# Image 1's returned rows on two DMA queues, and two of its six sums on POOL

## The reference, cut to what matters

```
t = _to_tokens(x)                     # x: (2, 128, 48, 48) -> (2, 2304, 128)
t = t + _L1_ffn_ref(_ln_t(t), gate_w, gate_b, w1, w2, w3)
x = _from_tokens(t, x)
return x
```

## Time and profile before

| what | before |
|---|---|
| runs | 684.36, 678.06 and 683.85 us, median 683.85 us |
| profiled execution | 683.36 us, of which the span from the first to the last instruction is 681.3 us |
| mean granted TensorE clock | 0.905 |
| busy time: PE, POOL, DVE, ACT | 554.9, 408.2, 348.6, 342.1 us |
| chain that ended last, by engine | PE 56%, DVE 14%, POOL 9%, ACT 7%, DMA 3% |
| DMA moved | 72.15 MB |

### The profile page before, as it was taken

One profiled execution on the slowest core, in us unless ns is written; L12 is line 12 of the kernel. 1 busy time (PEld: TensorE's weight loads), 2 busy tenths in 40 slices (PEclk: granted clock), 3 DMA queues, 4 the chain that ended last, 5 costly groups with the idle time before them and its releaser, 6 DMA issues.

```text
span 681.3 us, 15719 instructions
## 1 busy us (share of the span) xinstructions
PE 554.9 (81%) x5422; PEld 468.6 (69%) x5423; DVE 348.6 (51%) x1021; ACT 342.1 (50%) x801; POOL 408.2 (60%) x468
## 2 busy tenths in 40 slices
PE   2477788778779999999999999959649729999960
PEld 2466667657547777677777678748639729999960
DVE  6977787846620171212001274784875405555563
ACT  4467668886547243674122552522515406666640
POOL 1568789767567388675333330037747777777771
PEclk9689999979869699999999988978978959999995
DMA  8452322212055455322219200001123123333457
GB/s 296 161 140 82 85 73 81 67 47 70 13 180 201 154 174 171 128 94 99 88 47 331 61 1 1 0 23 52 52 61 98 52 85 99 98 97 98 128 204 242
DMA packets 56288, 72.15 MB, mean 106 GB/s; under 512 B 9086, under 2 KB 46934, under 8 KB 55614
## 3 DMA queue, kind: packets, MB, share of 16 engines
q1 hardware_dynamic: 49374, 58.36, 27.5%
q0 software_dynamic: 5120, 10.57, 4.7%
q10 hardware_dynamic: 1728, 2.36, 0.9%
HBM read 55.83 MB, written 21.69 MB: 114 GB/s over the span
## 4 chain that ended last, share of the span: by engine, by line
PE 56%; DVE 14%; POOL 9%; issue 9%; ACT 7%; DMA 3%; SPq 1%; POOLq 0%; DVEq 0%; ACTq 0%
PE bank L836 12%; PE bank L798 9%; PE bank L781 8%; PE bank L902 7%; PE bank L847 6%; POOL gathered_or_att L580 3%; POOL padded_or_w L571 3%; ACT normed L947 2%; POOL gathered_or_att L589 2%; PE bank L325 2%; DVE ln_stats L1133 2%; PE bank L796 2%; PE bank L827 2%; PE bank L733 2%; PE bank L867 1%
## 5 line engine op out<-in xcount | busy, mean ns | idle before, releaser
L615 POOL TENSOR_TENSOR padded_or_w<-padded_or_w,gathered_or_att 128x384 f32<-128x384 f32 x96 | 95.4, 1000 | 80.7 <-ACT padded_or_w L1021 77.0
L632 POOL DMA_INDIRECT sorted_x<-normed,slot x72 | 71.2, 989 | 80.0 <-DVE slot L1395 51.4
L1021 ACT ACTIVATE padded_or_w<-bank,moe_b 128x384 f32<-128x384 f32 x96 | 55.3, 579 | 107.2 <-PE bank L781 107.1
L651 POOL DMA_INDIRECT returned<-gathered_or_att,home_of_slot x88 | 87.2, 991 | 26.8 <-issue 19.8
L798 PEld LDWEIGHTS bank<-moe_or_conv,padded_or_w 128*128 128x128 f32 x576 | 80.6, 197 | 30.9 <-issue 9.8
L798 PE MATMUL bank<-moe_or_conv,padded_or_w 128*128 128x128 f32 x576 | 83.9, 284 | 0.0
L781 PE MATMUL bank<-chan_major,moe_or_conv 128*128 128x384 f32 x192 | 82.7, 517 | 0.1
L671 PE MATMUL bank<-padded_or_w 64*64 64x64 f32 x1152 | 47.5, 233 | 27.3 <-issue 15.9
L1459 DVE TENSOR_TENSOR att_or_moe<-att_or_moe,bank 128x256 f32<-128x256 f32 x88 | 37.0, 420 | 61.2 <-ACT att_or_moe L1035 39.9
L671 PEld LDWEIGHTS bank<-padded_or_w 64*64 64x64 f32 x1152 | 41.5, 145 | 36.6 <-issue 32.8
L580 POOL TENSOR_TENSOR gathered_or_att<-gathered_or_att,score_max 128x384 f32<-128x384 f32 x48 | 39.9, 830 | 34.5 <-DVE score_max L1217 33.7
(11 more groups left out here) (214 smaller groups left out, 1122.8 us busy)
## 6 DMA issues: line engine op xcount, KB each, us to landing
gathered_or_att<-combine SPq DMA_DIRECT2D x24, 768.0 KB, 4.2
padded_or_w<-windows SPq DMA_DIRECT2D x192, 48.0 KB, 2.0
sorted_x<-in_pad_rows SPq DMA_DIRECT2D x22, 260.0 KB, 7.1
padded_or_w<-sorted_x SPq DMA_DIRECT2D x22, 260.0 KB
padded_or_w<-in_moe_w SPq DMA_DIRECT2D x8, 512.0 KB, 5.4
qy<-returned SPq DMA_DIRECT2D x6, 384.0 KB, 5.8
out<-residual ACTq DMA_DIRECT2D x12, 192.0 KB, 2.1
normed<-returned SPq DMA_DIRECT2D x6, 384.0 KB, 5.4
```

What stands on the lines that cost most here:

```text
L615: nc.gpsimd.tensor_tensor(HB[n % DRING], HB[n % DRING], GB_[k % 3][:, n % 4, :], ALU.mult).then_inc(S("gated"), 1)
L632: nc.gpsimd.indirect_dma_start(xs_dram, bass.IndirectOffsetOnAxis(ap=POS[b][:, k, t:t + 1], axis=0), TNR[b][:, t, :], None).then_inc(S(don ...
L651: nc.gpsimd.indirect_dma_start(yt_dram, bass.IndirectOffsetOnAxis(ap=HOMES[b][:, j:j + 1], axis=0), YR[k * RING + j % RING], None).then_in ...
L1021: nc.scalar.activation(HB[n % DRING], banks[HBANK[n % 2]][:, 0:DG], ACT.Gelu, bias=B1C[:, e:e + 1]).then_inc(S("gelu"), 1)
```

## The change: what it does

Only image 1's end is changed; image 0's loads, sums and stores are issued as before.

- SP issues the loads of groups 0, 2 and 4 alone. The loads of groups 1, 3 and 5 are issued by ACT, at the beginning of `store(1)`, so behind image 0's stores and ahead of image 1's. For that ACT now has the nine waits of `y_rows_out` too, and one for the scatter of image 1, since the loads go into the tile that this scatter reads.
- Groups 2 and 5 are summed by POOL in place of DVE, in a new phase behind POOL's last indirect DMA: the same two additions, with a wait for itself between them.
- DVE leaves these two groups out, and ACT waits for a second semaphore, `out_ready_pool`, ahead of their stores. The stores are issued in the order of the groups, as before.

```diff
+        BY_POOL = (2, 5)
+        def returned_group(b, g):
+            return yt_dram[2 * NT * b:2 * NT * (b + 1), :].rearrange("(p g n) c -> g p (n c)", g=NG, n=2 * TG)[g]
...
-                rows = yt_dram[2 * NT * b:2 * NT * (b + 1), :].rearrange("(p g n) c -> g p (n c)", g=NG, n=2 * TG)
-                for g in range(NG):
-                    sp.dma_start(YL[b][g], rows[g]).then_inc(S(f"y_back{b}{g}"), 16)
+                for g in range(0, NG, 1 + b):
+                    sp.dma_start(YL[b][g], returned_group(b, g)).then_inc(S(f"y_back{b}{g}"), 16)
...
+            def combine(b):
+                for g in BY_POOL if b else ():
+                    xt = XT[b][:, g * TG:(g + 1) * TG, :].rearrange("p t c -> p (t c)")
+                    pool.wait_ge(S(f"y_back{b}{g}"), 16)
+                    nc.gpsimd.tensor_tensor(xt, xt, YL[b][g][:, 0:DG], ALU.add).then_inc(S("half_sum"), 1)
+                    pool.wait_ge(S("half_sum"), BY_POOL.index(g) + 1)
+                    nc.gpsimd.tensor_tensor(xt, xt, YL[b][g][:, DG:2 * DG], ALU.add).then_inc(S("out_ready_pool"), 1)
...
             def store(b):
+                if b:
+                    act.wait_ge(S("scattered1"), 16 * TT)
+                    y_rows_out(act, b)
+                    for g in range(1, NG, 2):
+                        nc.scalar.dma_start(YL[b][g], returned_group(b, g)).then_inc(S(f"y_back{b}{g}"), 16)
                 for g in range(NG):
-                    act.wait_ge(S("out_ready"), b * NG + g + 1)
+                    by_pool = [h for h in BY_POOL if b and h <= g]
+                    if g in by_pool:
+                        act.wait_ge(S("out_ready_pool"), len(by_pool))
+                    else:
+                        act.wait_ge(S("out_ready"), b * NG + g + 1 - len(by_pool))
                     nc.scalar.dma_start(out[b, :, g * TG:(g + 1) * TG, :], XT[b][:, g * TG:(g + 1) * TG, :]).then_inc(S("out_stored"), 16)
...
             def combine(b):
                 for g in range(NG):
+                    if b and g in BY_POOL:
+                        continue
```

More of the change, by code:

```diff
@@ L652, in send_back @@
                                                  YR[k * RING + j % RING], None).then_inc(S(f"y_sent{k}"), 16)
-            run(A=lambda n: attend(att, n), TO=toeplitz, AN=add_normed, D=dense, XC=pad, RS=scatter, M=send_back)
+            def combine(b):
[5 more added lines that the diff above has]
+                    nc.gpsimd.tensor_tensor(xt, xt, YL[b][g][:, DG:2 * DG], ALU.add).then_inc(S("out_ready_pool"), 1)
+            run(A=lambda n: attend(att, n), TO=toeplitz, AN=add_normed, D=dense, XC=pad, RS=scatter, M=send_back, F=combine)
         @block.tensor
```

## The result

The changed kernel took 696.25 us (median of 4 runs, 689.02 to 699.11) against 682.88 us for the kernel before (4 runs): a ratio of 1.0184, 95% interval 1.0138 to 1.0231. Forecast were 683.6 us and 677.8 to 685.8. Measured once more, with 11 runs against 28, it was 1.0077 (1.0039 to 1.0115), +5.3 us. So the change costs time, and the two measurements differ in how much. Executions over 1.5% above the fastest of their kernel are left out of the ratios and kept in the medians.

What follows compares the result with a forecast made beforehand. Bound by image 1's loads until group 3, three groups on DVE and one store; last store issued at 678.8 in place of 679.0 us, then 2.3 us unchanged: -0.2 us, 683.6 us against the median, range 677.8 to 685.8.

Steps and rivals of the forecast that it cites:

- What bounds the kernel, and the 13.3 us that can be touched: From SP's first load of image 1 (668.0 us) to the span's end (681.3): loads, DVE's sums, one store; 2% of span.
- Loads issued by two engines: Image 1's loads: SP's last issue comes 1.4 us earlier, worth nothing by itself; ACT's three issues cost 3 x 0.34 us.
- Stores behind loads: Image 1's stores queue behind ACT's loads: loads keep about 415 GB/s, groups land in pairs, the last 1.6 us earlier.
- The two engines beside each other: POOL's sums beside DVE's: each POOL addition takes 0.17 us more, 1.11 us, and the chain ends at 678.8 us.
- the first rival: POOL's and DVE's sums of image 1 exclude one another: +1.4 us, 685.2 us; chance 0.20.
- POOL's last indirect DMA ends ahead of all this, and nothing is queued behind the sums: POOL's sums of groups 2 and 5: POOL is free before them and has no work after; group 5 would end at 678.2.
- from there to the end stay 2.3 us: From the last store's issue (678.8 in place of 679.0 us) to the kernel's end: unchanged at 2.3 us.
- The chance of 0.92 for a change within 1%: Whole kernel: chance 0.92 that the time stays within 1% (6.8 us), with 0.04 each for faster and slower.

Runs made afterwards that it cites:

- loads alone: Changed kernel with all sums on DVE, image 1's loads still issued by SP and ACT; 680.73 us against 682.64 for the kernel before, ratio 0.9973.
- the changed kernel with the added DRAIN: Changed kernel plus one DRAIN on POOL directly behind its last indirect DMA, ahead of its sums; 24.1 us from PE's last DRAIN to the end.
- an early DRAIN: Changed kernel plus one DRAIN on POOL ahead of image 1's scatter; 29.7 us from PE's last DRAIN to the end.

## Why the prediction was wrong, point by point

- *What bounds the kernel, and the 13.3 us that can be touched:* right up to the last store, wrong behind it. I read the end off the chain of waits. The chain of the kernel before did name POOL's DRAIN, in one line among POOL's last operations, and I passed over it:

```profile
659.61 1.36 POOLq L60
```

  The line gives the 1.36 us that lie on the chain and not the 15.68 that the DRAIN lasts; only the operations of line 60 show its end.
- *Loads issued by two engines:* right. SP and ACT issue together (671.2 and 671.3 us), at no cost that shows.
- *Stores behind loads:* right in the rate, wrong in the order, and worth less than I took it for. The rate holds. But the groups do not come in pairs: in the changed kernel SP's three loads land ahead of ACT's (us from issue to landing; first line SP's, second ACT's):

```profile
DMA to landing us min/median/max: 4.2/5.7/7.2
```
```profile
DMA to landing us min/median/max: 4.9/7.3/8.0
```

  Group 2 starts on POOL 677.4 - 671.2 = 6.2 us after the first load, as forecast (674.2 - 668.0), but group 3 starts on DVE 7.8 us after it, where I had it land together with group 2 and start at 6.5. Group 5 was in 680.2 - 671.2 = 9.0 us after the first load, where I had 8.1 and before it was 9.7. What the loads alone are worth hardly shows: from the first load to the end of DVE's last sum it is 10.4 us in both profiles of loads alone, and 10.5 to 11.0 in the five with all loads on SP and all sums on DVE. The Trainium skill, in "DMA: Bandwidth & Descriptors" (section "Issuing engines are not separate DMA queues"), lets a second issuer save only the issuing time. The times agree with that within their scatter (ratio 0.9973, with 1 in its interval). Whether the steadier rate comes from the order on ACT's queue or from the second issuer, no run tells.
- *The two engines beside each other:* mis-sized. I took 0.17 us more for each of POOL's additions and none that matters for DVE's. POOL's mean is 1.13 us against the 1.11 forecast, which is luck, since that price came from indirect DMAs. DVE's four additions take nearly twice as long, DVE ends last, and the last store comes 0.9 to 1.3 us later in place of 0.2 earlier. That is close to the first rival's +1.4 us, but part of it is group 3, which that rival has on time. From 679.05 to 683.10 us four additions of DVE and two of POOL begin, and 0.5 us are left of an earlier one of POOL: one after another they would take 4 x 0.545 + 2 x 0.94 + 0.5 = 4.6 us, side by side 2.2, and 4.05 passed. When POOL's four stood beside DVE's four, in the changed kernel with the added DRAIN, they took 5.2 us (683.24 to 688.45) against 5.9 in turns. So the engines mostly take turns here, as the Trainium skill says in "SBUF — State Buffer" (section "Who interferes with whom"), but by these times the exclusion is not quite whole.
- *"POOL's last indirect DMA ends ahead of all this, and nothing is queued behind the sums":* this step failed, and with it *"from there to the end stay 2.3 us"*. POOL's DRAIN was queued behind, 8.7 us long; before, it had ended 5.8 us ahead of SP's, and now it ends 5.8 us behind. It costs 5.9 us of the 7.9. That POOL "has nothing behind its last indirect DMA", as the description of the kernel has it, is true of the operations that the kernel writes and not of the end of its program.
- *The chance of 0.92 for a change within 1%:* it rested on the claim that a loss of 1% would need sums of twice their length. Every part that I named was bounded; the part that decided was not among them. By the tails (+6.8 to +7.9 us) the loss is about 1%, most of it not from the sums, and by the second measurement (0.77%) it would still count as within 1%: the change lies near the edge of that band, and the first measurement beyond it.

Open are two things. What a DRAIN works off, and why 8.7 us: it is long only behind indirect DMAs, is paid once, and neither their number nor an early DRAIN gives its length. And the first measurement's 12.6 us: the tail explains 6.8 to 7.9 of it. In the one of these four runs that has a profile, the work ahead of PE's DRAIN took 2.5 us more than in the profile before (661.1 against 658.6 us), though the change doesn't touch it. The two longest runs, of 698.8 and 699.1 us, have granted clocks of 0.892 and 0.878 and no profile, so that where their time went is not shown. In the second measurement, of 5.3 us, there is no such rest.

## What to carry to other kernels

Before work is moved to an engine that finishes early, look at what that engine still has to do after its last operation, and whether the time is covered: here an idle engine had 5.8 us to spare and not the 14.5 us that its last operation suggested (666.6 to 681.1 us). Ask for the lines on which the program's end is booked, and compare the end of the chain with the end of the span; when they part by more than the last store takes (2.3 us before, 8.6 after), look behind the last operation. And take additions of DVE and POOL that both read two operands from SBUF as work mostly in turns, not side by side.

## What the hardware did that I had not expected

POOL's DRAIN takes 0.2 us after ordinary operations, 0.3 after one indirect DMA, and 3.0 to 8.8 us when 36 to 160 of them came before, even when POOL's last operation had ended 12 us before. It is paid when the queue reaches it, and a second one with no indirect DMA in between takes 0.2 us again.
